# Attention scores as single tiles in a ring of three banks, and values normalised with channels on partitions by way of DRAM

## The reference

```python
x = x + _L0_attn_a_ref(_layernorm(x), w_qkv_a, b_qkv_a)      # windowed attention
x = x + _L0_ffn_ref(_layernorm(x), Wg, w1, w2)               # 16 experts
x = x + _L0_attn_b_ref(_layernorm(x), w_qkv_b, w_o)          # the block of this case
x = x + _L0_ffn_ref(_layernorm(x), Wg, w1, w2)

# inside _L0_attn_b_ref, per batch and head (s = 1024, d = 16)
scores = jnp.einsum('bhqd,bhkd->bhqk', q, k) * d ** (-0.5)
attn = jax.nn.softmax(scores, axis=-1) * (s / np.sqrt(s - 1.0))
out = jnp.einsum('bhqk,bhkd->bhqd', attn, v) * s ** (-0.5)
return out @ w_o.T * hid ** (-0.5)
```

## Time and profile before

| | us |
|---|---|
| median of 3 runs (lowest, highest) | 5751.51 (5750.79, 5752.28) |
| the profiled execution | 5750.62 |
| its span | 5748.9 |
| PE busy | 5428.0 (94%) |
| DVE busy | 4498.2 (78%) |
| ACT busy | 3566.0 (62%) |
| POOL busy | 1473.5 (26%) |

### The profile page before, as it was taken

How to read it: one execution, slowest core, us unless ns; L and a number is a source line. 1 busy time by engine, 2 the same in 40 slices (tenths; PEclk the granted TensorE clock), 3 DMA queues, 4 the chain that set the end, 5 groups by cost and what they waited for, 6 DMA issues and landing times. The chain is left out here.

```text
span 5748.9 us, 131254 instructions
## 1 busy us (share of the span) xinstructions
PE 5428.0 (94%) x50092; PEld 3660.4 (64%) x50092; DVE 4498.2 (78%) x7377; ACT 3566.0 (62%) x5406; POOL 1473.5 (26%) x1948
## 2 busy tenths in 40 slices
PE   7999668999989889999999999999999997799999
PEld 6777457999978734444444444444444444699998
DVE  7888695555557689999999999999999996755554
ACT  5777562333325458888888888888888886433332
POOL 4655453333310000111111111111111114533332
PEclk9999889999999989999999999999999998999999
DMA  2222482222229811121112111111211113222221
GB/s 74 78 84 78 137 259 77 88 93 93 89 96 333 310 56 49 58 60 57 57 59 60 57 56 60 59 57 56 60 58 57 57 54 104 75 89 93 95 86 49
DMA packets 317697, 512.58 MB, mean 89 GB/s; under 512 B 36442, under 2 KB 221156, under 8 KB 311152
## 3 DMA queue, kind: packets, MB, share of 16 engines
q1 hardware_dynamic: 291912, 441.44, 24.2%
q0 software_dynamic: 24576, 64.56, 3.5%
q10 hardware_dynamic: 808, 1.07, 0.1%
HBM read 338.59 MB, written 185.60 MB: 91 GB/s over the span
## 5 line engine op out<-in xcount | busy, mean ns | idle before, releaser
L1773 DVE TENSOR_REDUCE at_best<-at_psM 128x2 f32<-128x1024 f32 x2048 | 2430.7, 1221 | 227.5 <-PE at_psM L1830 214.3
L1729 ACT ACTIVATE at_p<-at_psE 128x1024 f32<-128x1024 f32 (+1 forms) x2688 | 2077.1, 824 | 529.5 <-PE at_psE L1846 515.7
L1846 PE MATMUL at_psE<-at_q,at_k 50*128 50x512 f32 x4096 | 1174.0, 436 | 7.5 <-ACT at_p L1729 6.3
L1830 PE MATMUL at_psM<-at_k,at_q 48*128 48x512 f32 x4096 | 1093.6, 458 | 37.5 <-DMA at_k<-scratch_qk 27.4
L1857 PE MATMUL at_psO<-at_p,at_v 128*17 128x256 f32 x16384 | 1109.9, 383 | 0.1
L1122 ACT ACTIVATE e_h_hi<-e_psH 128x512 fp32r<-128x512 f32 x512 | 306.7, 599 | 916.0 <-PE e_psH L90 864.4
L1846 PEld LDWEIGHTS at_psE<-at_q,at_k 50*128 50x128 f32 x4096 | 548.7, 185 | 462.4 <-issue 223.6
L1196 DVE SCALAR_TENSOR_TENSOR e_h_lo<-e_psH,e_h_hi 128x512 fp32r<-128x512 f32 x512 | 353.9, 691 | 595.9 <-ACT e_h_hi L1122 505.8
L1857 PEld LDWEIGHTS at_psO<-at_p,at_v 128*17 128x17 f32 x16384 | 364.1, 96 | 542.7 <-issue 345.4
L1830 PEld LDWEIGHTS at_psM<-at_k,at_q 48*128 48x128 f32 x4096 | 471.3, 185 | 312.2 <-DVE at_best L1773 147.2
L90 PE MATMUL e_psE<-e_w_hi,e_h_hi 128*128 128x256 f32 x2048 | 583.1, 285 | 0.0
(11 more groups left out here) (213 smaller groups left out, 8456.5 us busy)
## 6 DMA issues: line engine op xcount, KB each, us to landing
e_w_raw<-in_w SPq DMA_DIRECT2D x64, 1024.0 KB
scratch_qk<-cp_qkh SPq DMA_DIRECT2D x64, 512.0 KB
scratch_qk<-cp_qkl SPq DMA_DIRECT2D x64, 512.0 KB
at_q<-scratch_qk SPq DMA_DIRECT2D x256, 128.0 KB
at_k<-scratch_qk SPq DMA_DIRECT2D x252, 128.0 KB
scratch_v<-cp_va SPq DMA_DIRECT2D x32, 544.0 KB
at_v<-scratch_v SPq DMA_DIRECT2D x126, 136.0 KB, 10.0
a_x<-in_x SPq DMA_DIRECT2D x32, 512.0 KB
```

The source lines that it names most:

```text
L1729: nc.scalar.activation(P[:, u:u + n, :], src, ACT.Exp, scale=HD ** -0.5).then_inc(p_ready, 1)
L1773: nc.vector.reduce_max(best[j % 2][:, h, :, qt], psM[h][:], AX_X).then_inc(m_taken, 1)
L1830: last = nc.tensor.matmul(psM[h][:, a, :], Q[j][r, 128 * qt:128 * qt + 128], K[j][r, 512 * h:512 * h + 512], start=True, stop=True)
L1846: last = nc.tensor.matmul(psE[:, u - u0 if n == 2 else 2, :], K[j][r, 128 * kc:128 * kc + 128], Q[j][r, 512 * half:512 * half + 512], star ...
```

## The change

It has five parts.

1. `scratch_qk` is laid out as head, half of the tokens, part, channel, 512 tokens, in place of part, head, channel, 1024 tokens. The projection stores a group's queries and keys in 8 DMAs of 256 KB (one tile each) in place of 4 of 512 KB. The loads of the attention take 32 or 16 rows, each in two pieces of 2 KB.
2. Scores by key are 32 single tiles. The three banks of `psE` are a ring in which the output projection and the maxima take a turn of their own (`IN_TURN`, `bank`), and a user waits for the one three turns earlier (`wait_for_bank`). ACT runs 32 exponentials of 512 columns.
3. `turn_values`, `turn_out`, `take_out` and `normalise` go. ACT still copies `psO`, and the next pair's values may begin right after that. SP stores the copy in a DRAM scratch (`store_values`) and, four pairs later or more, loads 256 tokens of 8 heads with channels on partitions (`raw`) and the denominators spread over the 16 channels of each head (`den`): `load_unit`. DVE inverts `den` as a 128 x 256 tile (`invert`), once a pair, and POOL multiplies.
4. The order in `pair` is new: value blocks 3 to 7 of a pair now run inside the next one, where it was 6 and 7.
5. After the last pair, `divide_end` inverts and multiplies four such units.

```diff
-    qkb = qk.rearrange("r (b h) d n -> b r (h d) n", h=H)
+    qkb = qk.rearrange("(b c h) s r d n -> s b c r h d n", c=2, h=H // 2)
...
-                        sp.dma_start(row(qkb, i)[r, :, half].rearrange("(c p) n -> p c n", p=128), buf[s][:, cs, :].bitcast(F32)).then_inc(qkv_stored[s], 16)
+                        for c in range(2):
+                            sp.dma_start(row(qkb[s], i)[c, r], buf[s][:, 2 * part + c, :].bitcast(F32)).then_inc(qkv_stored[s], 16)
...
-    qkp = qk.rearrange("r (u x) d n -> u x r d n", x=2)
+    qkp = qk.rearrange("(u a) s r d n -> u a (r d) s n", a=2)
+    rows = ot.rearrange("(b k i) a (m w) c -> b k m (i a) w c", k=2, i=4, m=4)
...
-        OUT_AT, MAX_AT, VALUES_AT, NORM_AT = 1, 11, 3, 3
+        OUT_AT, MAX_AT, VALUES_AT, INVERT_AT = 19, 14, 14, 15
+        IN_TURN = [user for u in range(NU) for user in (["out"] if u == OUT_AT else ["max"] if u == MAX_AT else []) + [u]]
...
-                eng.dma_start(Q[j][r:r + 32, :].bitcast(F32), row(qkp, pp)[a, 0:2]).then_inc(qk_loaded[j], 16)
+                eng.dma_start(Q[j][r:r + 32, :].bitcast(F32), row(qkp, pp)[a, 0:32]).then_inc(qk_loaded[j], 16)
...
+            def store_values(p):
+                sp.wait_ge(oT_ready, p + 1)
+                sp.dma_start(ot[p].rearrange("a r c -> r a c"), OT[:].rearrange("r (a c) -> r a c", a=2)).then_inc(oT_stored, 16)
+            def load_unit(u, slot, b, k, m, needed):
+                sp.wait_ge(oT_stored, 16 * needed)
+                after(sp, ofT_ready, u - 1)
+                sp.dma_start(raw[slot][:], rows[b, k, m][:, 0:HD, :]).then_inc(unit_loaded[slot], 16)
+                sp.dma_start(den[slot][:], rows[b, k, m][:, HD:HD + 1, :].broadcast_to([8, HD, 256])).then_inc(unit_loaded[slot], 16)
...
+                nc.gpsimd.tensor_tensor(oT[slot][:], raw[slot][:], den[slot][:], ALU.mult).then_inc(ofT_ready, 1)
...
-                src = psE[:, 0:2, :] if n == 2 else psE[:, 2:3, :]
-                nc.scalar.activation(P[:, u:u + n, :], src, ACT.Exp, scale=HD ** -0.5).then_inc(p_ready, 1)
+                nc.scalar.activation(P[:, u, :], bank(pp, u), ACT.Exp, scale=HD ** -0.5).then_inc(p_ready, 1)
...
+            def invert(u, slot):
+                dve.wait_ge(unit_loaded[slot], 32 * (u // 2 + 1))
+                nc.vector.reciprocal(den[slot][:], den[slot][:]).then_inc(rden_ready, 1)
...
+            def divide_end(m):
+                span = slice(256 * m, 256 * m + 256)
+                dve.wait_ge(end_loaded[m], 32)
+                nc.vector.reciprocal(end_den[:, span], end_den[:, span]).then_inc(end_rden_ready, 1)
+                dve.wait_ge(end_rden_ready, m + 1)
+                nc.vector.tensor_tensor(end_raw[:, span], end_raw[:, span], end_den[:, span], ALU.mult).then_inc(end_oT_ready, 1)
...
+                last_values(3), keys(0), query(0, 1), keys(1), query(1, 2), keys(2), last_values(4, (0,))
+                last_values(4, (1,)), keys(3, 5), query(2, 5), keys(5), last_values(5, (0,))
+                keys(6), query(3, 7), keys(7), last_values(5, (1,)), query(4, 8), keys(8, 11), last_values(6)
+                query(5, 11), keys(11, 13), query(6, 13), keys(13), last_values(7)
+                next_max_rows(), query(7, 14), keys(14, 16), query(8, 16), keys(16), values(pp, pb % 4, 0)
+                keys(17, 19), query(9, 19), output(), keys(19), query(10, 20), keys(20), query(11, 21)
+                keys(21), values(pp, pb % 4, 1, (0,)), keys(22, 24), values(pp, pb % 4, 1, (1,)), query(12, 24), keys(24), query(13, 25)
+                keys(25, 27), values(pp, pb % 4, 2, (0,)), keys(27), query(14, 28), keys(28), values(pp, pb % 4, 2, (1,))
+                keys(29), query(15, 30), keys(30, 32)
```

More of the change, by code:

```diff
@@ L1372, in group @@
             def group(g, s, i):
-                after(act, qkv_stored[s], 80 * i)
+                after(act, qkv_stored[s], 144 * i)
                 for c in range(4):
@@ L1477, in _, with attention_stage @@
             groups(pe, NG, group)
-def attention_stage(nc, T, stage, x, qk, v, woT, out):
+def attention_stage(nc, T, stage, x, qk, v, ot, woT, out):
     N, D = x.shape
@@ L1654, in _ @@
             batches(pair)
+            store_values(NP - 1)
+            sp.wait_ge(oT_stored, 16 * NP)
+            for m in range(4):
+                span = slice(256 * m, 256 * m + 256)
+                sp.dma_start(end_den[:, span], rows[B - 1, 1, m][:, HD:HD + 1, :].broadcast_to([8, HD, 256])).then_inc(end_loaded[m], 16)
+                sp.dma_start(end_raw[:, span], rows[B - 1, 1, m][:, 0:HD, :]).then_inc(end_loaded[m], 16)
             store_out(NP - 9, B - 2, PB - 1)
@@ L1697, in pair @@
             def pair(pp, pb, b):
+                if there(pp + 1):
+                    split_max(pp + 1, (pb + 1) % 4, turn_of(pp, pb, b, -1) + 1 if not first(pp) else 0)
                 if has_out(pp):
@@ L1832, in scores_by_query, with wait_for_bank @@
                 last.then_inc(m_done, 1)
-            def max_rows(p, j):
+            def wait_for_bank(pp, user):
+                n = turn_at_bank(pp, user) - BANKS
+                while n >= 0:
+                    pp, before = n // len(IN_TURN), IN_TURN[n % len(IN_TURN)]
+                    if before == "out" and has_out(pp):
+                        return pe.wait_ge(y_scaled, pp - 8)
+                    if before == "max" and there(pp + 1):
+                        return pe.wait_ge(nm_ready, pp + 2)
+                    if before != "out" and before != "max":
+                        return pe.wait_ge(p_ready, NU * pp + before + 1)
+                    n = n - 1
@@ L1890, in _ @@
                 if m == 20:
-                    max_rows(0, 0)
+                    max_rows(0, 0, psE[:, 2, :])
             pe.wait_ge(nm_ready, 1)
@@ L1900, in query, with keys @@
                         scores_by_query(mp, mj, turn_of(pp, pb, b, 1 if m // 2 < KC - LEAD else 2), qt, m % 2,
-                                        (GROUPS[g][0] + GROUPS[g][1]) % 2)
-                def key(g):
-                    if g == OUT_AT and has_out(pp):
-                        pe.wait_ge(y_scaled, pp - 8)
-                    if g == MAX_AT and there(pp + 1):
-                        pe.wait_ge(nm_ready, pp + 2)
-                    if g == MAX_AT and has_turned(pp):
-                        pe.wait_ge(xo_taken, pp - 3)
-                    scores_by_key(pp, pb % 4, turn_of(pp, pb, b, 0), g)
+                                        u % 2)
+                def keys(u, end=0):
+                    for each in range(u, max(u + 1, end)):
+                        scores_by_key(pp, pb % 4, turn_of(pp, pb, b, 0), each)
                 def last_values(kc, heads=(0, 1)):
@@ L1934, in pair @@
-                output(), query(0, -1), key(0), last_values(6)
-                query(1, 0), query(2, 0), key(1), key(2), last_values(7)
-                key(3), query(3, 3), key(4)
-                if not first(pp):
-                    turn_values(pp - 1)
-                key(5), query(4, 5), query(5, 5), key(6), values(pp, pb % 4, 0)
-                key(7), query(6, 7), key(8), values(pp, pb % 4, 1)
-                key(9), query(7, 9), key(10), query(8, 10), turns(), values(pp, pb % 4, 2, (0,))
@@ L1942, in pair @@
[L1942 to L1946 removed]
+                        project_out(ub, n, bank(pp, "out"))
```

195 lines of the change are left out of this document (90 added, 105 removed).

## The result

The changed kernel takes 5911.77 us (median of 4 runs, 5901.25 to 5921.94), the kernel before 5751.9 beside it: a ratio of 1.0275, 95% interval [1.0256, 1.0295]. It is slower by 160 us; the forecast was 5971. The profiled execution is the longest of the four (5921.94), so differences inside the trace add up to 171 us, not 160.

The account below looks back on a forecast made before the run. PE and DMA both bound the projection, PE's stream the attention pair, with DVE close behind. 5750.6 + 145 (stores) - 12 (start) + 77 (pairs) + 10 (end) + 0.9 = 5971.5 us; range 5905 to 6060, wider 5822 to 6075.

Parts of the forecast that it names:

- The projection's stores: Projection: stores with outermost dimension 8 run on eight engines, a group takes 14.0 us instead of 9.48, +145 us.
- The signs named: Projection: GB/s near 225, DMA share near 0.6, groups 14 us apart, PE near 70% busy, ACT waiting for `qkv_stored`.
- rival 4: Projection: PE's granted clock may fall once PE idles, up to +60 us more, 6030 us; chance 0.06.
- The attention's start: Attention's first loads: outer dimensions of 32 and 16 let all engines share them, -12 us.
- The inversion: DVE, once a pair: inverting 128 x 256 takes 1.8 us, between maximum 15 and the next pair's maximum 0.
- The stand at query 2: PE in the attention: query 2 waits for maximum 0, held up by the inversion, 0.8 us a pair.
- PE in a pair: PE's blocks in an attention pair sum to 21.05 us against 21.2, -0.15 a pair.
- the twelfth bundle: PE in a pair: one more bundle of score matmuls than before, costing 0.40 us for going in and out.
- Rival 3: Attention: the 0.40 us are waits for `psE` banks that the ring removes, -1.4 us a pair, 5718 us; chance 0.08.
- the attention's term: Attention pairs: the stall at query 2 with PE's -0.15 makes +0.65 us over 120 pairs, +77 us.
- ACT and the detour: Attention: ACT's 32 exponentials and the values' way through DRAM hold nobody up, both costed at nothing.
- The end: After the last copy of `psO`: 20.4 us to the last output instead of 10.1, +10 us.

Follow-up runs that it names:

- Experiment 2: Kernel before, its queries and keys stored in 8 DMAs of 256 KB with outermost dimension 8, forced by a spare row per head: 5908.98 us, ratio 1.0258.
- experiment 4: Kernel before, its loads of queries and keys cut into twelve transfers of 16 rows a pair, none with outer dimension 2: 5742.19 us, ratio 0.9979.
- experiment 5: Kernel of experiment 3, but only 16 of the 256 columns of denominators inverted, so the output is not the reference's: 5676.3 us, ratio 0.9863.
- experiment 3: Changed kernel with a scratch layout storing each tile as 128 plain rows, loads of 16 rows each: 5762.68 us, ratio 1.0012 to the kernel before.

## Why the prediction was right, and where it was not

**The projection's stores: right, slightly too cheap.** Forecast 14.0 us a group and +145; measured (2149.5 - 1695.7) / 31.75 = 14.29 us and 31.75 x (14.29 - 9.48) = +153, plus 9 us because the last group's stores drain for longer before the attention (10.7 us before, 19.9 after). The signs named are there: 216 GB/s for 225, a share of 0.63 for 0.6, ACT waiting for a DMA of the group (122.8 us, 29 times). Experiment 2 shows that the outermost dimension does it. The rule of the Trainium skill (DMA: Bandwidth & Descriptors, why a DMA increments its semaphore by 16), by which the engine count is the largest number up to 16 that divides the outermost dimension of both sides, fits here with 8 (a share of 0.63, where eight full engines and eight at a fifth make 0.6) as it did with 2; the share is a mean, and no row counts the engines one by one. Part of rival 4 came true as well, since the granted clock fell to 0.85 once PE had gaps; but PE had 24% of idle time, and 14.29 us lie inside the bounds of 13.7 and 15.1 that the engines' rate alone gave.

**The attention's start: right.** -12 forecast, -12.0 measured, and experiment 4 shows the cause, with -11.4 by itself.

**The inversion: right in place and nearly in size.** 1.74 us for 1.8: 16, 64 and 256 columns take 0.242, 0.543 and 1.742 us in these runs, some 6.2 ns a column. The 2.1 us that the prediction estimated from the repeat count of 8 in the Trainium skill (VectorE: DVE Perf Modes, the walkthrough of the 8-slice pipeline) are not borne out. The stand at query 2 is there in PE's timeline of the kernel after; its row, and the bundle behind the next value block:

```profile
3003.97 0.51 PE L1878 MATMUL at_psM<-at_k,at_q 48*128 48x512 f32 x2 [0.41 <-DVE at_best L1817]
...
3008.31 0.50 PE L1878 MATMUL at_psM<-at_k,at_q 48*128 48x512 f32 x2
...
3009.45 1.06 PE L1915 MATMUL at_psO<-at_p,at_v 128*17 128x256 f32 x16
```

The price by experiment 5 is 0.63 us a pair, for 0.80.

**PE in a pair: the step that failed.** The prediction took the cost of a bundle as "0.107 us per matmul and 0.40 us for going in and out", so that the twelfth bundle cost 0.40. Its two rows do not give these numbers: 1.14 us for 7 and 0.95 for 5 make 0.095 and 0.47. And bundles of other sizes are cheaper than the rule. PE's timeline of the kernel after, a bundle of 4 between two half value blocks, and one of 2:

```profile
3005.20 0.50 PE L1905 MATMUL at_psE<-at_q,at_k 50*128 50x512 f32 x1
3005.20 0.49 PE L1878 MATMUL at_psM<-at_k,at_q 48*128 48x512 f32 x1
3005.53 0.39 PE L1905 MATMUL at_psE<-at_q,at_k 50*128 50x512 f32 x1
3005.54 0.40 PE L1878 MATMUL at_psM<-at_k,at_q 48*128 48x512 f32 x1
3005.86 0.63 PE L1915 MATMUL at_psO<-at_p,at_v 128*17 128x256 f32 x8
3016.41 0.50 PE L1905 MATMUL at_psE<-at_q,at_k 50*128 50x512 f32 x2
3016.84 0.63 PE L1915 MATMUL at_psO<-at_p,at_v 128*17 128x256 f32 x8
```

They take 0.66 and 0.43 us, where the rule gives 0.83 and 0.61; those of 5 take 0.90 (the median) and those of 7 take 1.14. The kernel before has the same sizes at the same cost: a bundle of 4 ahead of its output projection, from these rows, takes 0.67.

```profile
3014.41 0.50 PE L1846 MATMUL at_psE<-at_q,at_k 50*128 50x512 f32 x2
3014.75 0.40 PE L1830 MATMUL at_psM<-at_k,at_q 48*128 48x512 f32 x2
3015.08 0.39 PE L90 MATMUL at_psE<-at_w_hi,at_oT_hi 128*128 128x256 f32 x1
```

The score matmuls start two by two (3005.20 and 3005.20, 3005.53 and 3005.54), and 0.43, 0.66, 0.90 and 1.14 us for 1, 2, 3 and 4 such twos are an estimated 0.20 us for going in and out and 0.23 for each two, an odd matmul counting as a whole two. A pair has 36 twos in either kernel. The largest bundle before holds 8 matmuls and takes 1.61 us, 0.5 more than four twos; inside it weight loads wait for a maximum and for an exponential. PE and its weight loads of the kernel before:

```profile
3011.82 0.50 PE L1846 MATMUL at_psE<-at_q,at_k 50*128 50x512 f32 x1
...
3012.41 0.19 PEld L1830 LDWEIGHTS at_psM<-at_k,at_q 48*128 48x128 f32 x2 [0.30 <-DVE at_best L1773]
...
3013.00 0.18 PEld L1846 LDWEIGHTS at_psE<-at_q,at_k 50*128 50x128 f32 x1 [0.29 <-ACT at_p L1729]
```

Summed by their start times over the whole pairs between 2400 and 4400 us, the blocks of PE come to these us a pair (the mean of this stretch lies 0.05 to 0.09 above that of all 127):

| | before | after | experiment 5 |
|---|---|---|---|
| value blocks | 8.03 | 8.29 | 8.28 |
| turns | 1.06 | 0.20 | 0.21 |
| output projection | 0.91 | 0.90 | 0.90 |
| bundles of score matmuls | 11.33 (11 of them) | 11.98 (12) | 11.31 (12) |
| the pair | 21.33 | 21.36 | 20.70 |

The turns (-0.86) and the halves (+0.25) came as forecast. The bundles were forecast at +0.40 and came to -0.02 without the stand, and that is nearly all by which the term was -0.65 in place of -0.15. That the prediction's sum still came to 21.2 for the 21.29 before is partly luck, since the constant that was too large stood in for waits. By the estimate the twelfth bundle costs 0.2, and the waits inside bundles fell by as much, from some 0.8 us a pair to some 0.6. Rival 3 took the 0.40 for such waits and forecast 1.4 us a pair. They exist, but the missing turns alone are worth more than the 0.65. Whether the ring or the new order shortened the waits is not separated by these runs. The stand adds 0.67 to the bundles of the kernel after, all of it in the one with query 2.

So the attention's term fails by its price of PE: the pairs gave -2 us for +77, of which 0.5 x 120 = 60 are the pair's term and 0.17 x 120 = 20 the stand's.

**ACT and the detour at nothing: right.** ACT is 84% busy, and the matmuls by key stand 4.0 us in the whole stage, 3.8 of them for ACT and none for the maxima's DMA. **The end: +12.5 for +10.** The inversions of 1.75 us stand behind one another there.

**The sum.** Forecast +145 - 12 + 77 + 10 = +220; measured in the trace +162 - 12 + 6 + 12.5 + 3 = +171, and by the medians +160. The time lies inside the range of 5905 to 6060, but near its lower end: the projection's term, the larger one, held, and the attention's +77 came to nothing.

## What to carry to other kernels

When a DRAM layout is changed, read the outermost dimension of each DMA side in the new code before anything else: 8 in place of 128 cost 153 us here with equal bytes and rows, and a layout with 128 plain rows gave it all back. A broadcast belongs behind the arithmetic, not ahead of it: inverting each denominator once and spreading the result through DRAM took 1.5 us a pair off DVE for two small DMAs. A sum of block times that fits the measured pair is no proof of its terms: here one constant too large stood in for waits inside the bundles. Take such a constant from blocks of several sizes, the smallest among them, before pricing one block more by it.

## What was not expected of the hardware

A short stand of PE can cost more than its length. In the doubled inversion the granted clock was still 1.00 while PE stood for 2.01 us, and was 0.50 afterwards; a full value block then took 1.91 us in place of 1.06. PE's timeline of that kernel:

```profile
3005.66 1.91 PE L1918 MATMUL at_psO<-at_p,at_v 128*17 128x256 f32 x16
```

Between 2400 and 4400 us the clock's mean was 0.84, and an estimated 383 of the 601 us over experiment 3 are its (601 less 1.70 x 128, the longer inversion priced one for one). With a stand of 1.21 us in each pair the mean stayed at 0.99.
